# First self attention of a two-layer decoder: the values' product in three fp32r terms and in new places, the queries and keys begun earlier, narrower waits for the banks

## The reference, cut to what matters

```python
def _L0_attn_ref(x, wq, wk, wv, wo):          # x is 4 x 1024 x 256
    xq = jnp.einsum('bsh,oh->bso', x, wq)     # 1024 outputs
    xk = jnp.einsum('bsh,oh->bso', x, wk)
    xv = jnp.einsum('bsh,oh->bso', x, wv)
    xq = xq.reshape(bsz, N_HEADS, seqlen, HEAD_DIM)   # and xk, xv: no transpose
    scores = jnp.einsum('bhid,bhjd->bhij', xq, xk) * SCALE
    scores = jax.nn.softmax(scores, axis=-1)
    out = jnp.einsum('bhij,bhjd->bhid', scores, xv)
    out = out.reshape(bsz, seqlen, N_HEADS * HEAD_DIM)
    return jnp.einsum('bso,ho->bsh', out, wo)
x = _layernorm(x + _L0_attn_ref(x, L0_attn_wq, L0_attn_wk, L0_attn_wv, L0_attn_wo), axis=-1)
```

## Time and profile before

| | |
|---|---|
| median of three runs | 3148.97 us |
| lowest and highest | 3145.57, 3155.68 us |
| the profiled execution | 3148.84 us, of which the span is 3146.8 us |
| mean granted TensorE clock over the span | 0.942 of full speed |
| TensorE matmul busy | 2768.1 us (88%) |
| VectorE, ScalarE, GpSimd busy | 1647.8, 1162.4, 1675.5 us |
| first self attention | about the first 1840 us |

### The profile page before, as it was taken

One profiled execution on the slowest core, in us unless ns is written; L12 is line 12 of the kernel. 1 busy time (PEld: TensorE's weight loads), 2 busy tenths in 40 slices (PEclk: granted clock), 3 DMA queues, 4 the chain that ended last, 5 costly groups with the idle time before them and its releaser, 6 DMA issues. The chain is left out here.

```text
span 3146.8 us, 41859 instructions
## 1 busy us (share of the span) xinstructions
PE 2768.1 (88%) x11637; PEld 1671.0 (53%) x11637; DVE 1647.8 (52%) x3266; ACT 1162.4 (37%) x1622; POOL 1675.5 (53%) x1418
## 2 busy tenths in 40 slices
PE   7999999999999999999999958871998388588686
PEld 4565555565556656555555533441997244334354
DVE  4555555555556555556555525651111555357843
ACT  2444434434334443434434324440111334245334
POOL 2666666666666666666666822226775512222343
PEclk9999999999999999999999989985999589799798
DMA  4233332233232233332333220013786200000143
GB/s 134 66 73 74 75 78 66 68 78 78 68 80 66 66 78 75 78 71 66 76 73 75 54 84 2 2 65 113 242 249 198 65 0 1 28 2 9 26 129 96
DMA packets 151406, 237.95 MB, mean 76 GB/s; under 512 B 30198, under 2 KB 75550, under 8 KB 151326
## 3 DMA queue, kind: packets, MB, share of 16 engines
q1 hardware_dynamic: 126510, 166.81, 21.4%
q0 software_dynamic: 20864, 64.06, 6.6%
q10 hardware_dynamic: 3952, 6.08, 0.6%
HBM read 89.52 MB, written 29.38 MB: 38 GB/s over the span
## 5 line engine op out<-in xcount | busy, mean ns | idle before, releaser
L620 POOL TENSOR_TENSOR a_total<-a_total,a_pr 128x1024 f32<-128x1024 f32 x384 | 908.7, 2366 | 78.2 <-ACT a_pr L604 54.1
L556 DVE TENSOR_REDUCE a_nmax<-a_psX 128x1 f32<-128x512 f32 x1024 | 695.0, 687 | 152.0 <-PE a_psX L551 149.8
L604 ACT ACTIVATE a_pr<-a_psS 128x1024 f32<-128x1024 f32 x512 | 524.5, 1025 | 487.4 <-PE a_psS L592 482.9
L632 PE MATMUL a_psO<-a_pr,a_vd 128*64 128x512 f32 x2048 | 481.8, 602 | 0.0
L551 PE MATMUL a_psX<-a_kA,a_qA 128*128 128x512 f32 x1024 | 418.6, 410 | 9.4 <-ACT a_vg L466 5.4
L620 POOL TENSOR_TENSOR a_total<-a_pr 128x1024 f32<-128x1024 f32 x64 | 152.8, 2388 | 413.5 <-ACT a_pr L604 413.5
L592 PE MATMUL a_psS<-a_qA,a_kA 128*128 128x512 f32 x1024 | 351.8, 425 | 0.2 <-ACT a_pr L604 0.2
L592 PE MATMUL a_psS<-a_qB,a_kB 128*128 128x512 f32 x1024 | 320.3, 394 | 0.0
L632 PEld LDWEIGHTS a_psO<-a_pr,a_vd 128*64 128x64 f32 x2048 | 130.0, 136 | 248.7 <-issue 218.8
L551 PEld LDWEIGHTS a_psX<-a_kA,a_qA 128*128 128x128 f32 x1024 | 192.8, 188 | 107.7 <-issue 27.4
L592 PEld LDWEIGHTS a_psS<-a_qA,a_kA 128*128 128x128 f32 x1024 | 185.5, 189 | 103.1 <-issue 73.7
(11 more groups left out here) (353 smaller groups left out, 4101.3 us busy)
## 6 DMA issues: line engine op xcount, KB each, us to landing
a_qA<-a_qhi SPq DMA_DIRECT2D x256, 128.0 KB, 2.3
a_kA<-a_khi SPq DMA_DIRECT2D x128, 128.0 KB, 2.3
a_kA<-a_klo SPq DMA_DIRECT2D x128, 128.0 KB, 2.3
a_kB<-a_khi SPq DMA_DIRECT2D x128, 128.0 KB, 2.3
a_qB<-a_qlo SPq DMA_DIRECT2D x128, 128.0 KB, 2.3
a_vd<-a_vg SPq DMA_DIRECT2D x128, 128.0 KB, 2.3
sorted_in<-g_zero SPq DMA_DIRECT2D x4, 1280.0 KB
e_xg<-sorted_in SPq DMA_DIRECT2D x40, 128.0 KB, 4.3
```

Source lines behind the costliest of these rows:

```text
L556: w.eng.tensor_reduce(nmax[:, half, u:u + 1], psX[:, half, :], AX.X, ALU.max, negate=True)\
L604: w.eng.activation(pr[:, n, :], psS[:, half, :, :].rearrange("p a b -> p (a b)"), ACT.Exp, scale=SCALE)\
L620: w.eng.tensor_tensor(total[:, buf, :], first, pr[:, n, :], ALU.add).then_inc(sems["ad"], 1)
L632: last = w.eng.matmul(psO[q * HD:(q + 1) * HD, :], vd[:, b, kc, :], pr[:, n, q * 512:(q + 1) * 512], start=kc == 0, stop=kc == KC - 1)
```

## The change

It has four parts.

- The value weights are held as two fp32r tensors (`wvh`, the rounded part, made by ScalarE before `walk`; `wvl`, the rest, made by VectorE behind the first two `build`s), and so is the transposed input (`xh`, `xl`). A `V` piece becomes six fp32r products of 512 columns: `xh` with `wvh`, `xh` with `wvl`, `xl` with `wvh`. `T` has one more copy on ScalarE and one subtraction on VectorE.
- Pieces move. `V` goes to new places "k6" (head 0), "k1" (head 1), "k6" and "k7" (head 2), behind the second `largest` of that kc. `T` goes to "3" and `O` to "3b" of head 2. The queries and keys of a group begin at head 3 of the group before the one that they began in: five pieces there ("1", "3", "3b", "3c", "3d"), three in head 0, five in head 1, three in head 2 ("1", "2", "2b"). Five of them are added before group 0. Places "2" and "2b" are used in head 2 alone, and head 0 has no "3d".
- The smaller of the two halves goes to `nT` in SBUF and not back to `psX` bank 0 (new semaphore `mn`). `largest` at i = 0 and the piece in "3c" wait for `mn`, the piece in "2b" for `mxr`, the piece in "3b" for neither; only `scores` waits for `mb`.
- `taken` waits for all copies into buffers 1 and for all but the newest into buffers 0, and is left out in the pieces before group 0. The `T` piece of group 1 stands ahead of the maxima of head 0.

```diff
--- before.py
+++ after.py
@@ -315,13 +315,14 @@
         wk = m.sb("wk", [P, 2, SEG * HD])
-        wv = m.sb("wv", [P, 2, SEG * HD])
+        wvh, wvl = (m.sb(n, [P, 2, SEG * HD], F32R) for n in ("wvh", "wvl"))
         xT = m.sb("xT", [P, 2, GT])
+        xh, xl = (m.sb(n, [P, 2, GT], F32R) for n in ("xh", "xl"))
@@ -336,7 +337,7 @@
-        nT = m.sb("nT", [KC, P])
+        nT = m.sb("nT", [KC, 2, P])
@@ -356,24 +357,23 @@
...
         def task_list():
 
-            qk = [("Q", c) for c in range(KC)] + [("K", c) for c in range(KC)]
-            places = [(0, "1"), (0, "2"), (0, "2b"), (0, "3b"), (0, "3c"), (0, "3d"),
-                      (1, "1"), (1, "2"), (1, "2b"), (1, "3"), (1, "3b"), (1, "3c"), (1, "3d"),
-                      (2, "1"), (2, "2"), (2, "2b")]
-            slots = dict(zip(places, qk, strict=True))
-            slots[0, "3"] = slots[2, "3"] = ("O",)
-            for n, place in enumerate(((2, "3b"), (2, "3c"), (3, "3"), (3, "3b"))):
+            slots = dict(zip(PLACES, QK, strict=True))
+            slots[0, "3"] = slots[2, "3b"] = ("O",)
+            slots[2, "3"] = ("T",)
+            for n, place in enumerate(((0, "k6"), (1, "k1"), (2, "k6"), (2, "k7"))):
                 slots[place] = ("V", n // 2, n % 2)
-            slots[3, "3d"] = ("T",)
             return slots
 
+        QK = [("Q", c) for c in range(KC)] + [("K", c) for c in range(KC)]
+        PLACES = [(3, "1"), (3, "3"), (3, "3b"), (3, "3c"), (3, "3d"), (0, "1"), (0, "3b"), (0, "3c"),
+                  (1, "1"), (1, "3"), (1, "3b"), (1, "3c"), (1, "3d"), (2, "1"), (2, "2"), (2, "2b")]
         SLOTS = task_list()
 
         def load_x(w, g):
@@ -389,11 +389,12 @@
 
         def taken(w):
 
-            for b in range(2):
-                w.wait(f"a{b}", w.at(f"a{b}", 8 * 16))
-                w.wait(f"b{b}", w.at(f"b{b}", 4 * 16))
-
-        def misc(w, what, G, buf, more=True, bank=None, back=(0, 0)):
+            w.wait("a0", w.at("a0", 8 * 16))
+            w.wait("b0", w.at("b0", 4 * 16))
+            w.wait("a1", w.at("a1"))
+            w.wait("b1", w.at("b1"))
+
+        def misc(w, what, G, buf, more=True, bank=None, back=(0, 0), fresh=False):
 
 
             kind = what[0]
@@ -417,11 +418,12 @@
                                             start=cc == 0, stop=cc == 1)
                 elif kind == "V":
                     _, tt, c2 = what
-                    if tt == 0 and c2 == 0:
-                        w.wait("wv", 16)
-                    for cc in range(2):
-                        last = w.eng.matmul(ps[:, :], xT[:, cc, tt * P:(tt + 1) * P],
-                                            wv[:, cc, c2 * 512:(c2 + 1) * 512], start=cc == 0, stop=cc == 1)
+                    w.wait("wl", 1)
+                    w.wait("xl", w.at("xl"))
+                    for n, (xp, wp) in enumerate(((xh, wvh), (xh, wvl), (xl, wvh))):
+                        for cc in range(2):
+                            last = w.eng.matmul(ps[:, :], xp[:, cc, tt * P:(tt + 1) * P], wp[:, cc, c2 * 512:(c2 + 1) * 512],
+                                                start=n == 0 and cc == 0, stop=n == 2 and cc == 1)
                 elif kind == "S":
                     w.wait("ad", w.at("ad", 3 if more else 0))
                     for q in range(2):
@@ -437,7 +439,15 @@
             if kind == "T":
                 if w.on("scalar"):
                     w.wait("mi", w.at("mi"))
+                    w.wait("xl", w.at("xl"))
                     w.eng.activation(xT[:, :, :].rearrange("p a b -> p (a b)"), ps[:, :], ACT.Copy).then_inc(sems["ma"], 1)
+                    w.eng.activation(xh[:, :, :].rearrange("p a b -> p (a b)"), ps[:, :], ACT.Copy).then_inc(sems["ma"], 1)
+                if w.on("vector"):
+                    w.wait("ma", w.at("ma", -2))
+                    w.eng.tensor_tensor(xl[:, :, :].rearrange("p a b -> p (a b)"), xT[:, :, :].rearrange("p a b -> p (a b)"),
+                                        xh[:, :, :].rearrange("p a b -> p (a b)").bitcast(F32), ALU.subtract).then_inc(sems["xl"], 1)
+                w.inc("xl")
+                w.inc("ma")
             elif kind in "QK":
                 hi, lo = (qhi, qlo) if kind == "Q" else (khi, klo)
                 c = what[1]
@@ -447,14 +457,14 @@
                     v = t[:, bass.ds(buf, 1), :, c * HD:(c + 1) * HD]
                     return v.rearrange("p b h t -> p (b h) t")
                 if w.on("scalar"):
-                    if what == ("Q", 0):
+                    if what == ("Q", 0) and not fresh:
                         taken(w)
                     w.wait("mi", w.at("mi"))
                     w.eng.activation(dst(hi), src, ACT.Copy).then_inc(sems["ch"], 1)
                 w.inc("ch")
 
                 if w.on("vector"):
-                    if what == ("Q", 0):
+                    if what == ("Q", 0) and not fresh:
                         taken(w)
                     w.wait("ch", w.at("ch"))
                     w.eng.tensor_tensor(dst(lo), src, dst(hi).bitcast(F32), ALU.subtract).then_inc(sems["md"], 1)
@@ -543,7 +553,7 @@
             if w.on("tensor"):
                 if i == 0:
                     w.wait(f"a{b}", w.at(f"a{b}"))
-                    w.wait("mb", w.at("mb"))
+                    w.wait("mn", w.at("mn"))
                 if i in (0, 13):
                     w.wait("md", w.at("md", back[0]))
                     w.wait("ma", w.at("ma", back[1]))
@@ -568,13 +578,15 @@
             w.inc("mt")
             if w.on("vector"):
                 w.wait("mt", w.at("mt"))
-                w.link(w.eng.tensor_copy(nT[:, :], psX[0:KC, 0, 0:P]), "dv")
-                w.link(w.eng.tensor_tensor(psX[0:KC, 0, 2 * P:3 * P], nT[:, :], psX[0:KC, 0, P:2 * P], ALU.min), "dv")
+                w.link(w.eng.tensor_copy(nT[:, 0, :], psX[0:KC, 0, 0:P]), "dv")
+                w.eng.tensor_tensor(nT[:, 1, :], nT[:, 0, :], psX[0:KC, 0, P:2 * P], ALU.min).then_inc(sems["mn"], 1)
+                w.wait("mn", w.at("mn", -1))
                 w.eng.tensor_tensor(qB[0:KC, b, :].rearrange("p (u q) -> p u q", q=P),
-                                    psX[0:KC, 0, 2 * P:3 * P].unsqueeze(1).to_broadcast([KC, KC, P]), rowmask[:, :, :], ALU.mult)\
+                                    nT[:, 1, :].unsqueeze(1).to_broadcast([KC, KC, P]), rowmask[:, :, :], ALU.mult)\
                     .then_inc(sems["mb"], 1)
             else:
-                w.inc("dv", 2)
+                w.inc("dv")
+            w.inc("mn")
             w.inc("mb")
 
         def scores(w, kc, b, a):
@@ -676,16 +688,14 @@
 
                 def piece(where, bank=None, under=(0, 0)):
 
+
                     task = SLOTS.get((j, where))
                     if task is None or (last and task[0] != "O") or (not old and task[0] == "O"):
                         return under
                     if task[0] == "O":
-                        misc(w, task, G - (j == 0), 1 if j == 0 else 0)
+                        misc(w, task, G - (j == 0), 1 if j == 0 else 0, bank=bank, back=under)
                     else:
-                        if bank is not None and w.on("tensor"):
-                            w.wait("mxr", w.at("mxr"))
-                            w.wait("mb", w.at("mb"))
-                        ahead = 2 if task[0] == "T" else 1
+                        ahead = 2 if task[0] == "T" or j == 3 else 1
                         misc(w, task, G + ahead, (G + ahead) % 2, bank=bank, back=under)
                     return (under[0], under[1] + 1) if task[0] in "TV" else (under[0] + 1, under[1])
 
@@ -700,6 +710,7 @@
                         if kc == KC - 1 and not (last and j >= 2):
                             build(w, (G + (j + 2) // GH) % 2, (j + 2) % GH, b)
                         step(2 * kc + 1)
+                        piece(f"k{kc}")
                         if old and kc == 4:
                             turn_back(w)
                         if old and kc == 5:
@@ -714,7 +725,10 @@
                         if p == 1 and more:
                             build_v(w, (j + 1) % GH, nb)
                     if p == 2:
-                        piece("2b", bank=psX[:, 1, :], under=piece("2"))
+                        under = piece("2")
+                        if w.on("tensor") and (j, "2b") in SLOTS:
+                            w.wait("mxr", w.at("mxr"))
+                        piece("2b", bank=psX[:, 1, :], under=under)
                 for kc in range(KC - 4, KC):
                     values(w, kc, b)
                 take_out(w)
@@ -722,6 +736,8 @@
                     max_rows(w, nb)
                 first_d, first_a = under = piece("3")
                 under = piece("3b", bank=psX[:, 1, :], under=under)
+                if w.on("tensor") and (j, "3c") in SLOTS:
+                    w.wait("mn", w.at("mn"))
                 under = piece("3c", bank=psX[:, 0, :], under=under)
                 piece("3d", under=(under[0] - first_d, under[1] - first_a))
                 if j % 2 == 0 and old:
```

(19 more changed lines are left out.)

## The result

The changed kernel is **slower**: 3165.17 us, median of nine executions (3160.75 to 3171.43), beside 3145.57 for the kernel before on the same chip (nine, 3138.78 to 3155.68). The ratio is 1.0062, with a 95% interval of 1.0048 to 1.0075: +19.6 us, where -23 was forecast. The profiled execution of the changed kernel has a span of 3169.4.

The account below looks back on a forecast made before the run. TensorE, busy 109.92 of a group's 111.52 us, was taken as the bound. From 3148.84, -34.5 (15 groups at -2.3) and +12.0 before group 0 gave 3126 us; its own range was 3112 to 3138.

Parts of the forecast that it names:

- Value arithmetic: Value pieces in the loop: 6.88 us of fp32 work removed, 5.57 of fp32r products added, -1.3 per group.
- The waits for `mb`: Tails of heads 1 and 3: TensorE's lost waits for the bank, 1.24 and 0.38 us, go; -1.6 per group.
- waits only move: Rival: the `mb` waits move to "3d", behind VectorE's subtraction for "3"; 1.2 + 0.4 us per group returns, 3150; chance 0.08.
- The wait at kc 6: `largest` at i = 13 no longer waits for the "2b" piece's evacuation in heads 0 and 1; -0.5 us per group.
- Tail of head 0: It ends with "3c", so the first `largest` waits for that piece's evacuation; +0.83 us per group, bounds 0.5 and 1.0.
- Tail of head 2: `largest` waits for VectorE's addition of `O` instead of ScalarE's last value copy, a step of the same size; zero.
- Value pieces' waits: Value pieces among the scores add TensorE waits between fp32r runs; between zero and 1.4 us per group, taken as +0.3.
- The rival in which they are dear: Value pieces cost what entering and leaving an fp32 burst costs, 0.34 us each; +16 us, 3142; chance 0.14.
- Copies of `build`: Copies that `largest` needs in the tails of heads 1 and 3 keep about 1.0 us of margin; cost zero.
- the rival that had them bind: Copies of `build` become the bound in the tails of heads 1 and 3; slower, 3158 to 3170 us; chance 0.07.
- Before group 0: Exposed start: +4.0 us for rounding value weights, +3.0 for value pieces and `T`, +5.0 for five query pieces; +12.0, bounds 8 and 16.

## Why the prediction was wrong

By its own steps, per group:

- *Value arithmetic, -1.3*: **right**, -1.36 in the timeline (4 x 0.34) and 1.52 between the two kernels that differ in it.
- *The waits for `mb`, -1.6*: **the step that failed**. It said of "3d": "by the same rows that write ends 2.1 after the transposes". In the earlier trace rows that write reads PSUM; the change moves that input to SBUF, and the prediction carried the duration over. It found that "3d" "just fits", by 0.06, and the write became 0.96 longer. What was removed (1.24 and 0.38 per group) came back as 0.79 and 0.83, so the step is worth 0.0 in place of -1.6. The rival *waits only move* has the right place and, by its sum, nearly the right price (1.6), but it was given 8 in 100 because of a margin computed with the wrong duration. The Trainium skill, "SBUF — State Buffer", section "SBUF: two separate sides", has the rule: VectorE and GpSimd share a pair of ports that is "an **exclusive lock**, not a bandwidth split", taken by a VectorE operation with two inputs in SBUF, against a GpSimd operation that reads SBUF. The trace agrees: the write waits for GpSimd's end and then takes 1.08, and never less than 1.21 in all. By it the two inputs in SBUF spoke against this change, and the prediction did not weigh it.
- *The wait at kc 6, -0.5*: right; the wait for VectorE's subtraction is gone in heads 0 and 1 and stays in head 2.
- *Tail of head 0, +0.83*: right, 0.93.
- *Tail of head 2, zero*: **wrong twice**. The text counted `T`'s second copy as "hidden behind the `O` piece", and it was hidden, but its second increment of `ma` was not followed to those who count: +0.93, and 1.02 came back when it was counted. And "a step of the same size" was not quite one: +0.35.
- *Value pieces' waits, +0.3*: zero. The rival in which they are dear falls.
- *Copies of `build`*: no idle time of a `largest` is ended by them; zero, as forecast, and the rival that had them bind falls. The waits that move give 3150 by their own sum; the rest came from the tail of head 2, which no rival named.

The sum is -1.36 + 0 - 0.5 + 0.93 + 0.93 + 0.35 = +0.35, where 111.84 - 111.52 = +0.32 is measured. Between this and -2.3 stand 1.6 of the write, 0.93 of the count, 0.35 of head 2's last wait, 0.1 of head 0's and -0.3 of the waits that cost nothing, 2.7 in all; times 15 that is some 40 us, the distance between the forecast and the measured time.

*Before group 0, +12.0*: right in sum, 12.3 up to group 1, but by luck, since two errors cancel. The first query piece is later by 3.8 (4.0 forecast); the value pieces start 35.40 - 28.38 = 7.0 later; the maxima's transposes 10.5, not 7; the first score 17.8, not 12. Against that, group 0 gives 5.5 back, which the prediction did not have; why was not pursued. The clock was 0.50 up to some 65, for nearly all of the four query pieces, after VectorE's reductions had kept TensorE waiting, where the prediction had that clock for two of them: the first score comes 8.4 behind the transposes (59.45 to 67.86). It was 0.50 from 36 to 40 as well, behind an idle time of 3.33 in which TensorE waited for `wvl`, where the value pieces before the change ran at 1.00: up to 40.66 their pairs of products start 0.85 apart and later 0.46, which makes 2.5 of the 3.5 that the maxima's transposes are later than forecast.

Shown by experiments: the lock (input in PSUM, or GpSimd idle, each alone), the count, the price of the value products, of the start and of the tail of head 0. Only read from timelines: the +0.35 of head 2, the clock of the value pieces, and why the write in head 1's tail meets an addition in one kernel and not in the other.

## To carry to other kernels

When a change moves an operand from PSUM to SBUF, the instructions that read it get a new price: look up what GpSimd is doing at that moment, and add its remaining time. When a piece gains an instruction that signals, follow the increment to each place that counts such pieces, since a wait one too far costs as much as a real dependency. And a margin of less than a tenth of a microsecond, as here, is no margin: what hangs on it should be priced both ways before it is given a small chance.

## What was not expected of the hardware

- A VectorE operation on 8 partitions with both inputs in SBUF, 1.21 alone, becomes up to 2.65 when it meets GpSimd's addition over 128 partitions: the small size of the operand does not spare it. When it starts during the addition, it ends 1.08 after the addition's end, in all 33 such cases of the changed kernel. With one input in PSUM it takes 1.21 even when it starts during an addition, in all 33 such cases of that run.
- Three products in fp32r, six instructions with four waits ahead of them, among scores in fp32r, start without a gap: 0.23 each throughout.
- The same kernel before took 3145.57 on one chip and 3177.72 to 3184.79 on the others, and the changed kernel 3165.17 and 3195.16. The last block of its self attention began at 1846.9 and 1846.6 in these two, so the difference lies in the blocks that follow. So only runs of one chip, or ratios, are compared here.
